# Decoder block: the memory product of the first attention as one matmul per head, with a third load of v

## The reference

```python
def step(carry, qkv):
    mem, zc = carry
    qs, ks, vs = qkv
    sq = jax.nn.elu(qs) + 1.0
    mem = mem + jnp.einsum('bhsk,bhsv->bhkv', sq, vs)
    zc = zc + (jax.nn.elu(ks) + 1.0).sum(axis=-2, keepdims=True)
    scores = jnp.einsum('bhsk,bhtk->bhst', qs, ks) * scale
    att_dot = jnp.einsum('bhst,bhtv->bhsv', jax.nn.softmax(scores, axis=-1), vs)
    num = jnp.einsum('bhsk,bhkv->bhsv', sq, mem)
    den = sq.sum(axis=-1, keepdims=True) * zc
    att = gate * (num / den) + (1.0 - gate) * att_dot
    out_seg = att.reshape(Bx, L, H * DV) @ Wo
    return ((mem, zc), out_seg)
```

## Time and profile before

| | |
|---|---|
| median of 3 runs | 1166.75 us (1165.61 to 1181.71) |
| the profiled execution, own time | 1170.84 us |
| its span | 1169.0 us |
| TensorE busy | 942.4 us, 81% |
| VectorE busy | 771.5 us, 66% |
| ScalarE busy | 568.4 us, 49% |
| GpSimd busy | 366.7 us, 31% |
| queue of SP, GpSimd's queue (share of 16 engines) | 52.1%, 1.3% |
| mean granted clock of TensorE | 0.905 |

### The profile page before, as it was taken

How to read it: one execution, slowest core, us unless ns; L and a number is a source line. 1 busy time by engine, 2 the same in 40 slices (tenths; PEclk the granted TensorE clock), 3 DMA queues, 4 the chain that set the end, 5 groups by cost and what they waited for, 6 DMA issues and landing times. The chain is left out here.

```text
span 1169.0 us, 27086 instructions
## 1 busy us (share of the span) xinstructions
PE 942.4 (81%) x9501; PEld 800.7 (68%) x9502; DVE 771.5 (66%) x1249; ACT 568.4 (49%) x1247; POOL 366.7 (31%) x371
## 2 busy tenths in 40 slices
PE   5798898989889898988989898989968955039960
PEld 4687787878778787877878787877755644029950
DVE  7577877767787776768686776768646855014428
ACT  4455565555556555556556465555532211027750
POOL 3222323222233322222233222222223410736652
PEclk9699999999999998999899899989899975559985
DMA  6657656666765666675655566676620660140114
GB/s 208 151 124 161 142 128 144 144 153 137 160 140 130 144 144 144 134 155 141 144 126 126 130 144 155 134 148 134 162 53 28 177 91 0 50 112 31 31 41 127
DMA packets 181141, 144.05 MB, mean 123 GB/s; under 512 B 72176, under 2 KB 167184, under 8 KB 174976
## 3 DMA queue, kind: packets, MB, share of 16 engines
q1 hardware_dynamic: 178464, 139.06, 52.1%
q0 software_dynamic: 2656, 4.72, 1.3%
HBM read 83.83 MB, written 59.94 MB: 123 GB/s over the span
## 5 line engine op out<-in xcount | busy, mean ns | idle before, releaser
L322 POOL TENSOR_TENSOR ps<-s_exp,row_rec 128x512 f32<-128x512 f32 x64 | 65.5, 1044 | 481.8 <-DVE row_rec L734 481.8
L350 PEld LDWEIGHTS bank<-psT,lhs 128*64 128x64 f32 x2048 | 137.0, 145 | 100.7 <-issue 88.4
L350 PE MATMUL bank<-psT,lhs 128*64 128x64 f32 x2048 | 153.7, 232 | 53.9 <-DMA lhs<-scratch_vg 53.0
L659 DVE TENSOR_TENSOR lhs<-bank,zg_all 64x512 f32<-64x512 f32 x128 | 88.9, 694 | 142.7 <-PE bank L414 141.3
L414 PE MATMUL bank<-pos_qv 128*64 128x64 f32 (+1 forms) x2048 | 162.2, 228 | 0.0
L414 PEld LDWEIGHTS bank<-pos_qv 128*64 128x64 f32 (+1 forms) x2048 | 140.2, 137 | 24.3 <-issue 10.9
L602 ACT ACTIVATE psT<-bank 128x512 f32<-128x512 f32 x128 | 70.4, 595 | 164.4 <-PE bank L397 164.4
L535 ACT ACTIVATE attT<-bank 64x256 f32<-64x256 f32 x256 | 96.5, 377 | 60.5 <-PE bank L350 58.1
L314 POOL TENSOR_TENSOR vg_out<-qv_out,ungate 128x1024 f32<-128x1024 f32 x32 | 81.0, 2532 | 115.4 <-ACT qv_out L577 104.1
L526 ACT ACTIVATE s_exp<-s_exp 128x512 f32<-128x512 f32 x64 | 40.4, 631 | 131.5 <-DVE s_exp L727 131.5
L676 DVE SCALAR_TENSOR_TENSOR e_qk<-qk_tok,e_qk 128x1024 f32<-128x1024 f32 x32 | 88.2, 2756 | 1.1
(11 more groups left out here) (208 smaller groups left out, 1785.3 us busy)
## 6 DMA issues: line engine op xcount, KB each, us to landing
scratch_qv<-qv_out SPq DMA_DIRECT2D x32, 1024.0 KB, 3.9
pos_qv<-scratch_qv SPq DMA_DIRECT2D x64, 512.0 KB, 6.3
scratch_vg<-vg_out SPq DMA_DIRECT2D x32, 512.0 KB, 4.5
zg_all<-scratch_z SPq DMA_DIRECT2D x32, 512.0 KB, 4.8
lhs<-scratch_vg SPq DMA_DIRECT2D x64, 256.0 KB, 8.3
sorted_x<-padding SPq DMA_DIRECT2D x1, 2515.5 KB, 21.1
r_all<-in_x_dram SPq DMA_DIRECT2D x4, 512.0 KB, 6.0
cx<-in_ctx_dram SPq DMA_DIRECT2D x8, 256.0 KB, 2.9
```

Of the source, the lines that this page charges most:

```text
L350: last = pe.matmul(mix_bank[f % 2][0:DK, i * L:(i + 1) * L], lhs[:, 1 - n, h, :], psT[:, h, n * L:(n + 1) * L], start=True, stop=True)
L659: dve.tensor_tensor(lhs[DK:, :, s, :].rearrange("p n h k -> p h n k"), mix_bank[f % 2][DK:, :].rearrange("p (h n k) -> p h n k", n=SEG, h= ...
```

## The change

`remember` makes one matmul per head and not two. Its stationary operand is as before sq of all 128 rows; its moving operand has 128 columns: v, and beside it a copy of v whose rows of the second segment are zero. The product with that copy is the sum over the first 64 rows. For this `pos_qv` gets 64 further columns per head. Their rows 64 to 127 are set to zero once for each of the two buffers, by GpSimd; their rows 0 to 63 are filled in every step by a third transfer of `pos_qv` (256 KB, pieces of 256 bytes), which SP issues behind the two others. The waits on `qv_loaded` count three transfers. v times (1 − gate) goes through DRAM as before.

```diff
-        pos_qv = [sb(f"pos_qv{i}", [P, H, 2 * DK]) for i in range(2)]
+        pos_qv = [sb(f"pos_qv{i}", [P, H, 3 * DK]) for i in range(2)]
...
                 for n in range(SEG):
                     src = scratch_qv[bass.ds(t, 1), n * L:(n + 1) * L]
-                    sp.dma_start(pos_qv[p][n * L:(n + 1) * L, :, :],
+                    sp.dma_start(pos_qv[p][n * L:(n + 1) * L, :, 0:2 * DK],
                                  src.rearrange("o (h j) c e -> (o j c) h e", j=J)).then_inc(qv_loaded[p], 16)
+                sp.dma_start(pos_qv[p][0:L, :, 2 * DK:],
+                             scratch_qv[bass.ds(t, 1), 0:L, :, DK:].rearrange("o (h j) c e -> (o j c) h e", j=J)).then_inc(qv_loaded[p], 16)
...
             pool.wait_ge(x_pad, 1)
+            for i in range(2):
+                pool.memset(pos_qv[i][L:, :, 2 * DK:], 0.0).then_inc(v_blanked, 1)
+            pool.wait_ge(v_blanked, 2)
             pool.wait_ge(xt_low, B // 4)
...
+                    if is_step(u, 0) and f == 0:
+                        pe.wait_ge(v_blanked, 2)
                     if f == 0:
-                        pe.wait_ge(qv_loaded[q], 32 * (hq + 1))
+                        pe.wait_ge(qv_loaded[q], 48 * (hq + 1))
...
-                    for n, k in ((0, P), (1, L)):
-                        for i in range(4):
-                            at = (2 * i + n) * DK
-                            last = pe.matmul(mix_bank[f % 2][DK:, at:at + DK], pos_qv[q][0:k, 4 * f + i, 0:DK],
-                                             pos_qv[q][0:k, 4 * f + i, DK:], start=True, stop=True)
+                    for i in range(4):
+                        at = 2 * i * DK
+                        last = pe.matmul(mix_bank[f % 2][DK:, at:at + 2 * DK], pos_qv[q][:, 4 * f + i, 0:DK],
+                                         pos_qv[q][:, 4 * f + i, DK:], start=True, stop=True)
                     last.then_inc(mem_ready, 1)
...
-                    dve.wait_ge(qv_loaded[q], 32 * (hq + 1))
+                    dve.wait_ge(qv_loaded[q], 48 * (hq + 1))
```

More of the change, by code:

```diff
@@ L206, in attention_phase @@
         tanh_ready, gate_ready = sem("tanh_ready"), sem("gate_ready")
-        x_pad, x_staged = sem("x_pad"), sem("x_staged")
+        x_pad, x_staged, v_blanked = sem("x_pad"), sem("x_staged"), sem("v_blanked")
         k_proj, q_proj, v_proj = sem("k_proj"), sem("q_proj"), sem("v_proj")
```

## The result

The changed kernel takes 1201.61 us (median of 4 runs, 1197.52 to 1210.35), against 1174.23 us for the kernel before over all runs that count here (1165.61 to 1182.04). The ratio is 1.0205, with a 95% interval of 1.0151 to 1.0259: slower, by more than the noise. Whether by more or by less than 2% these runs do not say. The profiled execution took 1202.92 us, 32 us more than the one of before. Between the `attend(0)` of image 0 and the one of image 29, 29 steps, lie 785.2 us (65.82 to 851.02), 27.08 us a step; in the kernel before the same stretch has 26.07 us a step. That is 29 of the 32 us; of the rest, 1.8 us lie before this stretch and 1.1 us behind it, so the other phases hardly changed.

A forecast was written before the change was run, and what follows sets the result against it. A three-leg ring through the lhs wait was taken as the bound. Steps of 25.2 us at full clock and 27.0 after clock falls averaged 26.4, × 30 = 792 against 780, +12, giving 1179 us; range 1153 to 1210.

The forecast's parts named there:

- What bounds the kernel: Attention loop: three legs in a ring hold two steps at 51.2 us; TensorE waits for the lhs transfer before attend.
- Matmuls: In remember on TensorE: half the instructions, saving 1.1 us a step (estimates 0.96 to 1.26).
- The added load: Third pos_qv load on SP's queue ahead of the lhs loads: cannot hide, costs 1.7 us with SP's issue.
- S to A: Leg from issue of the scratch_qv store to start of attend(0): from 15.3 to 17.0 us.
- The bound of 2.75 us by pieces: Upper bound for the third load's cost, if each piece costs the same whatever its size.
- The waits on qv_loaded: VectorE's sq_sum and remember(0) wait for three loads, the third landing 13.7 us after the store's issue: costed at nothing.
- the cover: Margin between the third load's landing and VectorE's sq_sum needing it: 2 us.
- T to S: VectorE's leg from start of the w_k projection to issue of the scratch_qv store: 13.2 us, or 14.4 with GpSimd overlap.
- The clock: TensorE's longer idle waits lower its clock: a fall in two of three steps, before one in four.
- The ring of one step from A to A: From one attend(0) start to the next after a clock fall: 9.9 + 0.1 + 17.0 = 27.0 us.
- A to T: TensorE's leg from start of attend(0) to start of the w_k projection: from 21.3 to 20.2 us at full clock.
- The load decides: Rival: the queue before attend(0) dominates, through falls in every step or a dearer load; mostly 1190 to 1212, chance 0.29.

The follow-up runs named there:

- mm_only: Kernel before with one 128-column matmul per head but no third load (memory product not the reference's): 1171.08 us, ratio 0.9934.
- lhs_early: Changed kernel with the two lhs loads issued right behind the store of q and v, ahead of its wait and all pos_qv loads: 1140.9 us.
- load_only: Changed kernel with the two matmuls per head of before, keeping the third load and wider pos_qv: 1227.37 us, ratio to before 1.0456.
- load512: Changed kernel with its third load replaced by another 256 KB in 512-byte pieces into a spare buffer, pos_qv at its old width: 1210.47 us.
- third_behind: Changed kernel with the third pos_qv load issued behind the two lhs loads, not ahead of them: 1206.17 us.
- pool_after: Changed kernel with one more GpSimd wait, so L319 begins only after VectorE has written sq: 1187.11 us.
- best: Changed kernel with lhs loads issued early, L319 held until sq is written, and a separate semaphore for the third load: 1088.26 us.

## Why the prediction was right, and where it was not

The time fell into the range (1153 to 1210) and no change or slower by a little was the way forecast; but the likeliest value, 1179, was 23 us low. Of these, 7 us are the base: the forecast started from 1166.75 us, and the kernel before took 1174.23 us over all runs here. The other 15 us are in the difference: +12 us forecast, +27 us between the medians. The range held it in its slower half, which was meant for other mechanisms (falls in every step, a dearer load), and that is luck.

- *What bounds the kernel*: right. The wait for `lhs` in front of `attend` is what mm_only and lhs_early show from both sides.
- *Matmuls*: right in size. A pair takes 1.89 us (457.80 to 459.69) against an estimate of 1.79 to 1.94 us, so 1.06 us a step, where 1.1 was taken. The prediction held that the trace does not separate what a change of rows costs from other causes. The start times of the single instructions do. In L414 of the kernel before, an instruction starts 58 ns after the one in front of it, but 152 or 148 ns after it where the rows change from 128 to 64 or back, and the next one 107 ns later. Three such places in a pair cost 0.43 us, most of the 0.53 us that the change saves there. L420 has none of them: 160 ns after its first instruction, then 109 ns throughout. TensorEngine Tiling (Array Packing) of the Trainium skill, section Tiling Modes, says that a change of mode drains the engine; the trace agrees, with 90 to 94 ns at the change and 49 ns behind it.
- *The added load*: right on its leg. 17.0 us from S to A, measured 16.8 to 17.1; load_only has the same. The bound of 2.75 us by pieces is refuted by it, and by load512. The page DMA: Bandwidth & Descriptors of the Trainium skill (section Specifications) asks for 512 B for the full rate; the load costs 1.67 us in pieces of 256 bytes and 1.50 us in pieces of 512, a small difference.
- *The waits on qv_loaded*: nearly right. 6.2 us in 8 times, where nothing was costed. The third load lands 13.4 to 13.7 us after S, as forecast (13.7). But `sq_sum` starts only 13.8 us after S in every second step, so the cover is 0.2 to 0.4 us there and not 2. third_behind and lhs_early use it up and pay 76.3 and 55.6 us.
- *The overlap of VectorE and GpSimd*: this step failed. The prediction read L684's 1.53 us for 0.69 us as a price of 0.84 us, and reckoned that a later L314 would free VectorE: T to S 13.2 us, "or 51.6 and 25.8 if L684 still lies under L314". L684 is free of it (L690, 0.68 us). The wait moved to the next instruction and grew: L696 takes 3.25 and not 1.23 us, so T to S is 15.2 us. This comes in 10 steps, about 21 us together; taking it away gave 14.5 us (pool_after).
- *The clock*: right in kind. The forecast had a fall in two of three steps; the lower level shows at 17 of 30 `attend(0)`, in most of the loop at every second one. The ring of one step from A to A, reckoned at 27.0 us after a fall, is 26.7 us (443.09 to 469.75). The next, 415.18 to 443.09 with the clock up at its start, is 27.9 us. The legs of two steps say why: 22.4 + 15.2 + 16.8 = 54.4 us, where 20.2 + 13.2 + 17.0 = 50.4 us were reckoned at full clock. A to T behind the fall gives 2.2 us of the difference (0.4 of them because the leg is 20.6 and not 20.2 us even at full clock) and the overlap 2.0 us. With a T to S of 13.2 us the same legs give 26.2 us a step, near the 26.4 of the forecast. One reading of the rows before was too broad: of the eight waits there from 449.70 us on, four were followed by an `attend(0)` of 1.94 us; at the others it took 1.37 to 1.74 us, and A to T 22.9 us and not 23.9.
- *The sum*: 26.4 us a step forecast, 27.08 measured, where 26.07 was the mark. Without the overlap, pool_after has 26.36.
- *The rivals*: "The load decides" had its mechanism right (the load alone costs 4.6%), and the kernel came out at its lower edge. It came there through the overlap on top of a fall in every second step, not through a fall in every step.

## What to carry to other kernels

Where two steps of a pipeline share a ring of legs, work taken from the engine that waits buys little (0.7% in mm_only), and a load put ahead of the one it waits for costs its full transfer time on that leg; move that load away, or issue the awaited one before, and the same saving counts (19.5 us here). Give a transfer a semaphore of its own when its readers differ: the wait of the reader that doesn't need it cost 44 us. And an overlap of two engines is to be priced at each instruction that can fall under it, not at the one that lies under it now.

## What the runs showed of the hardware

- A VectorE instruction of two kinds that starts while GpSimd's 128x1024 multiply runs is finished only after it. L696, with two inputs in SBUF, ends 1.09 us after L319 and takes 3.25 us in place of 1.23. A `TENSOR_SCALAR` with one input (L683 of mm_only) ends 0.54 us after L314 and takes 2.01 us in place of 0.68. A `TENSOR_REDUCE` is not held: L674 takes 1.22 us whether GpSimd's L327 (128x512) runs at its start, as in 14 steps, or not. The Trainium skill, Advanced Engine Details and Errata, section VectorE Performance Modes, says that VectorE's second SBUF port is shared with GpSimd, and that GpSimd's instructions and VectorE's two-port ones block each other. The trace agrees for the two kinds held, and shows a block up to GpSimd's end; in which mode they ran it does not show.
- The same price is paid in every step at a place that none of the kernels moved. L682 (L676 of the kernel before) takes 1.23 us for the first image, where GpSimd does nothing beside it, and 2.80 us in the 31 others, where it runs beside L310 and ends 1.1 us after it:

```profile
20.29 1.23 DVE L682 SCALAR_TENSOR_TENSOR e_qk<-qk_tok,e_qk 128x1024 f32<-128x1024 f32 x1
...
416.65 2.33 POOL L310 TENSOR_TENSOR ps<-pos_qv,sq_rec 128x1024 f32<-128x1024 f32 x1
...
417.26 2.81 DVE L682 SCALAR_TENSOR_TENSOR e_qk<-qk_tok,e_qk 128x1024 f32<-128x1024 f32 x1
```

It adds up to 88.2 us in the kernel before, the changed one and best alike, where 32 times 1.23 us would be 39. It lies in T to S; no run takes it away, so what it is worth in the total is open.
- The same load in 512 or in 1024 pieces lengthened S to A by 1.50 or 1.67 us for 256 KB, while the transfer engines were full (in the changed kernel a busy share of 1.39 and 157 GB/s from 440 to 441 us).
- The instructions of 128 moving columns with 64 weight columns (L420) start 109 ns apart, and so do those with 128 weight columns (L380 of the kernel before; the 112 ns of the earlier trace rows are a mean with the slower start of each group). Those of 64 moving columns (L350, L414) start 58 ns apart.
